# Moving the sums, the context and the next batch's x inside TensorE's order of a post-LN transformer block

## The reference

```python
q, k, v = split(x @ w_qkv)                      # 16 heads of 32
p   = softmax(q @ k.T / sqrt(512))              # all 1024 keys
x1  = layernorm(x + p @ v)
g   = fp4(x1) @ fp4(w_gate).T                   # 512 -> 1408
y   = fp4(x1) @ fp4(w_up).T
h   = silu(g) * y
out = layernorm(x1 + fp4(h) @ fp4(w_down).T)    # 1408 -> 512
```

## Time and profile before

| | us |
|---|---|
| median of 3 runs | 4034.84 (4033.22 to 4035.09) |
| the profiled execution | 4030.72 |
| its span | 4029.1 |
| set-up, up to the first weighing | 207.6 |
| one batch, from first weighing to first weighing | 478 to 480 |
| in it: first weighing to first gate of the FFN | 263 |

### The profile page before, as it was taken

How to read it: one execution, slowest core, us unless ns; L and a number is a source line. 1 busy time by engine, 2 the same in 40 slices (tenths; PEclk the granted TensorE clock), 3 DMA queues, 4 the chain that set the end, 5 groups by cost and what they waited for, 6 DMA issues and landing times. The chain is left out here.

```text
span 4029.1 us, 61264 instructions
## 1 busy us (share of the span) xinstructions
PE 3757.5 (93%) x22658; PEld 1726.6 (43%) x22853; DVE 3034.4 (75%) x4931; ACT 1711.7 (42%) x3085; POOL 2231.5 (55%) x1419
## 2 busy tenths in 40 slices
PE   3599999999999999999999999999999999999999
PEld 2243454334543445343444335433454344534344
DVE  9877787677866688667877778767786668866787
ACT  2166423653246622555226542356323552255522
POOL 1288523984258832687228852398425883268722
PEclk9699999999999999999999999999999999999999
DMA  4211101011011110101101110101101111011110
GB/s 164 79 35 33 53 22 36 17 42 47 24 30 29 36 45 19 40 26 33 48 24 36 33 53 19 38 17 41 48 24 31 29 36 45 19 38 27 33 48 22
DMA packets 106593, 152.83 MB, mean 38 GB/s; under 512 B 28176, under 2 KB 55568, under 8 KB 106128
## 3 DMA queue, kind: packets, MB, share of 16 engines
q1 hardware_dynamic: 106256, 148.49, 11.9%
HBM read 76.28 MB, written 19.66 MB: 24 GB/s over the span
## 5 line engine op out<-in xcount | busy, mean ns | idle before, releaser
L570 DVE TENSOR_REDUCE mx<-R 128x1 f32<-128x512 f32 x2080 | 1332.1, 685 | 567.3 <-PE R L662 561.0
L1191 ACT ACTIVATE arena<-SC 128x512 f32<-128x512 f32 x1344 | 747.8, 603 | 337.7 <-PE SC L1437 335.7
L1508 PE MATMUL SC<-wgu,split 128*128 128x512 f16 (+1 forms) x3456 | 715.9, 361 | 11.3 <-DVE split L1335 11.3
L1090 POOL TENSOR_TENSOR wd<-wd,arena 128x1024 f32<-128x1024 f32 x208 | 485.8, 2359 | 23.7 <-ACT arena L1191 22.6
L1116 POOL TENSOR_TENSOR arena<-arena,sc_h 128x704 f32<-128x704 bf16 (+2 forms) x136 | 176.1, 1312 | 577.0 <-DVE arena L495 577.0
L1508 PEld LDWEIGHTS SC<-wgu,split 128*128 128x128 f16 x3456 | 337.4, 98 | 345.6 <-DVE split L1335 13.2
L1191 ACT ACTIVATE wd<-SC 128x512 f32<-128x512 f32 x704 | 401.4, 604 | 195.9 <-PE SC L1437 185.6
L662 PE MATMUL R<-ks_even,qs_even 96*128 96x512 bf16 x1056 | 400.8, 395 | 57.1 <-issue 43.0
L1232 ACT ACTIVATE arena<-SC,gain 128x512 f32<-128x512 f32 (+1 forms) x192 | 125.0, 651 | 769.6 <-PE R L1508 396.2
L642 PE MATMUL R<-xT,wqkv 128*128 128x512 bf16 x1501 | 395.4, 381 | 28.9 <-DVE xT L557 14.8
L662 PE MATMUL R<-arena 96*128 96x512 bf16 x1024 | 373.8, 381 | 14.6 <-DVE xT L557 8.8
(11 more groups left out here) (138 smaller groups left out, 5332.1 us busy)
## 6 DMA issues: line engine op xcount, KB each, us to landing
x<-n_L_attn_embeddings_dram SPq DMA_DIRECT2D x136, 256.0 KB, 2.8
wd<-wd_kept SPq DMA_DIRECT2D x32, 512.0 KB, 5.1
out_dram<-x SPq DMA_DIRECT2D x64, 256.0 KB, 2.0
ks_even<-split SPq DMA_DIRECT2D x204, 64.0 KB, 2.0
qs_even<-split SPq DMA_DIRECT2D x408, 32.0 KB, 1.8
arena<-split SPq DMA_DIRECT2D x192, 64.0 KB, 2.0
arena<-split SPq DMA_DIRECT2D x384, 32.0 KB, 1.8
wd<-wd_kept SPq DMA_DIRECT2D x16, 384.0 KB, 6.9
```

Source lines behind the costliest of these rows:

```text
L570: nc.vector.reduce_max(mx[:, j:j + 1], ring_of(ring, job)[:, :], AX_X).then_inc(max_done, 1)
L1090: nc.gpsimd.tensor_tensor(acc[u % 2][i], first, probs_of(s)[:, hs, :], ALU.add).then_inc(pool_sum, 1)
L1191: nc.scalar.activation(probs_of(s)[:, hd, :], SC[e % SLOTS][:, :], ACT.Exp, scale=SCALE).then_inc(exp_done, 1)
L1508: last = nc.tensor.matmul(GU[kk % 2][which][:, 0:w], xhT[i % 2][:, part_x * KH + k, :], wgu[:, part_w * KH + k, which * I + first:which * ...
```

## The change

* The sum goes from step 1 to place 2 of step 2, ahead of the weighing; the turn of the sums from step 2 to ahead of the weighing of step 4, and the context's from step 3 to behind it. GpSimd's add follows one step later.
* The eight turns of the next batch's x go from one a step (steps 1 to 7 of unit 5, step 0 of unit 6) to two at a time, behind the weighings of steps 2, 4 and 6 of unit 5 and ahead of that of step 0 of unit 6. SyncE now loads all the tiles ahead of the maxima of unit 6.
* Two quarters of the last v projection go ahead of unit 7's last weighings; `neg` goes behind the turn of x's tile 0.
* First FFN tile: the turn of x tile 1 comes after the second chunk instead of the third; VectorE does the moments of tile 2 and the quantising of x tile 1 ahead of the context of unit 7, and quantises h by chunks, as the last tile does already; GpSimd follows.
* Set-up: the copy of w_down to HBM is issued after the last load of weights instead of between two of them.

```diff
--- before.py
+++ after.py
@@ -91,10 +91,10 @@
         ((3, (2, 3, 4)), (2, 2, 2, 1, 1, 1, 2, 1)), ((3, (5,)), (4, (0,)), (4, 0, 0, 0, 0, 1, 1, 2)),
         ((4, (1, 2, 3)), (0, 2, 2, 2, 2, 2, 2, 0)), ((4, (4,)), (1, 1, 1, 1, 0, 0, 0, 0)))
 SCORES_AT, VALUES_AT = (0, 1, 3, 4), 2
-SUM_STEP, SUM_T_STEP, CTX_STEP = 1, 2, 3
-ADD_TILE, ADD_TILE_LAST = 3, 2
+SUM_STEP, CTX_STEP = 2, 4
+ADD_TILE, ADD_TILE_LAST = 4, 3
 LN_MOMENTS, LN_SCALE = 5, 6
-X_TURNS = [(UNITS - 3, t) for t in range(1, TILES)] + [(UNITS - 2, 0)]
+X_TURNS = [(UNITS - 3, t) for t in (2, 2, 4, 4, 6, 6)] + 2 * [(UNITS - 2, 0)]
 def quarters(g, j):
@@ -115,23 +115,22 @@
     m = [("max", u + 1, n) for n in range(sum(counts[:t]), sum(counts[:t + 1]))]
     made, by_step = unit_projections(u)
     q = made[sum(by_step[:t]):sum(by_step[:t + 1])]
-    other = []
-    if u > 0:
-        other += [("sum", u - 1, 0)] if t == SUM_STEP else []
-        other += [("sumT", u - 1, 0)] if t == SUM_T_STEP else []
-        other += [("ctx", u - 1, 0)] if t == CTX_STEP else []
-    if (u, t) in X_TURNS:
-        other += [("xT", X_TURNS.index((u, t)), 0)]
+    before, behind = [], []
+    if u > 0 and t == SUM_STEP:
+        before = [("sum", u - 1, 0)]
+    if u > 0 and t == CTX_STEP:
+        before, behind = [("sumT", u - 1, 0)], [("ctx", u - 1, 0)]
+    turns = [("xT", n, 0) for n, step in enumerate(X_TURNS) if step == (u, t)]
     neg = [("neg", u + 1, 0)] if t == TILES - 1 and not ends else []
     if t == 0:
-        return m[0:1] + q[0:1] + m[1:2], m[2:3], [], m[3:4] + q[1:2], other, m[4:5] + q[2:] + m[5:]
-    return [], m[0:1] + q[0:1], m[1:2], neg + m[2:3] + other, m[3:4] + q[1:2], m[4:5] + q[2:] + m[5:]
+        return m[0:1] + q[0:1] + m[1:2] + turns, m[2:3], [], m[3:4] + q[1:2], [], m[4:5] + q[2:] + m[5:]
+    return [], m[0:1] + q[0:1], m[1:2] + before, turns + behind + neg + m[2:3], m[3:4] + q[1:2], m[4:5] + q[2:] + m[5:]
 def first_jobs():
     v = quarters(GROUPS, PROJ_JOBS - 1)
-    return ([("sum", UNITS - 1, 0), ("neg", UNITS, 0)] + v[0:2] + [("xhT", 0, 0)] + v[2:] + [("sumT", UNITS - 1, 0)],
+    return (v[0:2], [("sum", UNITS - 1, 0), ("xhT", 0, 0), ("neg", UNITS, 0)] + v[2:] + [("sumT", UNITS - 1, 0)],
             [("ctx", UNITS - 1, 0)])
@@ -139,7 +138,7 @@
     if i == 0:
-        return [], [], [("xhT", 1, 0)], []
+        return [("xhT", 1, 0)], [], [], []
     turns = [("hT", i - 1, n) for n in range(len(CHUNKS))]
     if i == TILES - 1:
         return turns[0:1], turns[1:2], turns[2:], [("hT", i, 0)]
@@ -349,12 +348,21 @@
         def pieces(i):
-            cols = H_PIECES if i < TILES - 1 else [chunk_cols(c) for c in range(len(CHUNKS))]
-            return [(len(H_PIECES) * i + n, c) for n, c in enumerate(cols)]
+            cols = [chunk_cols(c) for c in range(len(CHUNKS))] if in_chunks(i) else H_PIECES
+            before = len(H_PIECES) * i + (len(CHUNKS) - len(H_PIECES) if i > 0 else 0)
+            return [(before + n, c) for n, c in enumerate(cols)]
         def pieces_before(i, col):
-            return len(H_PIECES) * i + sum(c.start < col for _, c in pieces(i))
+            return pieces(i)[0][0] + sum(c.start < col for _, c in pieces(i))
+
+        def in_chunks(i):
+
+            return i in (0, TILES - 1)
+
+        def rounds_before(i):
+
+            return i + (len(CHUNKS) - 1 if i > 0 else 0)
         def chunk_cols(c):
             return slice(CHUNKS[c][0], CHUNKS[c][0] + CHUNKS[c][1])
@@ -800,8 +808,8 @@
                     if n == load_number[("round", DOWN_ROUNDS + 6)]:
                         for name in STACKS:
                             stack(GROUPS, name)
-                        sp.wait_ge(wT_done, 2 * DOWN_ROUNDS)
-                        sp.dma_start(wd_kept, wd[:, :, :]).then_inc(wd_saved, 16)
+                sp.wait_ge(wT_done, 2 * DOWN_ROUNDS)
+                sp.dma_start(wd_kept, wd[:, :, :]).then_inc(wd_saved, 16)
                 stack_maxima(UNITS)
                 stacks_done(sp, 1)
                 sp.wait_ge(m_loaded, 32)
@@ -1025,11 +1033,9 @@
                         if u == UNITS - 1:
                             stack(g, STACKS[2])
                         if u == UNITS - 3:
-                            for t in turns[:-1]:
+                            for t in turns:
                                 load_turn(t)
                         stack_maxima(u + 1)
-                        if u == UNITS - 3:
-                            load_turn(turns[-1])
                     def load_down(c):
@@ -1109,7 +1115,7 @@
                     def scale_h(i, n):
                         k, cols = pieces(i)[n]
-                        pool.wait_ge(rh_done, i + 1 + (n if i == TILES - 1 else 0))
+                        pool.wait_ge(rh_done, rounds_before(i) + 1 + (n if in_chunks(i) else 0))
                         if i >= 1:
                             pool.wait_ge(ring_full, ring.full(("hT", i - 1, (cols.stop - 1) // BANK)))
                         c = slice(cols.start // BLK, cols.stop // BLK)
@@ -1126,13 +1132,15 @@
                                 add(u - 1)
                     scale_x(0)
                     inverse_deviation("x", 1)
+                    inverse_deviation("x", 2)
+                    scale_x(1)
                     add(UNITS - 1)
                     for i in range(TILES):
-                        if i + 1 < TILES:
+                        if 1 <= i < TILES - 1:
                             scale_x(i + 1)
                         if 2 <= i < TILES - 1:
                             inverse_deviation("out", i - 2)
-                        if i + 2 < TILES:
+                        if 1 <= i < TILES - 2:
                             inverse_deviation("x", i + 2)
                         for n in range(len(pieces(i))):
                             scale_h(i, n)
@@ -1355,7 +1363,7 @@
                         first, w = CHUNKS[c]
                         dve.wait_ge(silu_done, k + 1)
                         if i >= 1 and c == 0:
-                            dve.wait_ge(rh_done, i)
+                            dve.wait_ge(rh_done, rounds_before(i))
                         nc.vector.scalar_tensor_tensor(h[:, first:first + w], GU[k % 2][1][:, 0:w], un_gain,
                                                        sg[:, k % 2, 0:w], ALU.mult, ALU.mult).then_inc(h_done, 1)
@@ -1367,26 +1375,31 @@
                         dve.wait_ge(y_added, i + 1)
                         moments("out", i, x1[:, i % 4, :], o_done)
+                    low_x(0)
                     maxima_transposed(UNITS)
-                    low_x(0)
                     reciprocals(UNITS - 1)
+                    first_moments(2)
+                    quantise_x(1)
                     context_out(UNITS - 1)
-                    for i in range(TILES - 1):
+                    for c in range(len(CHUNKS)):
+                        gated(0, c)
+                        if c == 1:
+                            low_x(1)
+                        dve.wait_ge(h_done, c + 1)
+                        quantise_h(0, chunk_cols(c))
+                    for i in range(1, TILES - 1):
                         gated(i, 0)
                         quantise_x(i + 1)
                         gated(i, 1)
-                        if i == 0:
-                            low_x(1)
-                        else:
+                        if i >= 1:
                             low_h(i - 1, 0)
                             if i >= 2:
                                 add_ffn(i - 2)
                                 second_moments(i - 2)
                             low_h(i - 1, 1)
                         gated(i, 2)
-                        if i >= 1:
-                            low_x(i + 1)
-                            low_h(i - 1, 2)
+                        low_x(i + 1)
+                        low_h(i - 1, 2)
                         if i + 2 < TILES:
                             if i == 2:
                                 dve.wait_ge(added, UNITS)
@@ -1489,6 +1502,7 @@
                                 weigh(s - 1)
                             if n in SCORES_AT:
                                 scores(u, t, SCORES_AT.index(n))
+                    run(first_jobs()[0])
                     weigh(len(steps) - 2)
                     weigh(len(steps) - 1)
@@ -1532,12 +1546,12 @@
                         if c == len(CHUNKS) - 1:
                             last.then_inc(y_done, 1)
-                    run(first_jobs()[0])
+                    run(first_jobs()[1])
                     for i in range(TILES):
                         places = tile_jobs(i)
                         gate_up(i, 0, 0)
                         if i == 0:
-                            run(first_jobs()[1])
+                            run(first_jobs()[2])
                         gate_up(i, 0, 1)
                         gate_up(i, 1, 0)
                         gate_up(i, 1, 1)
```

## The result

The changed kernel takes 3990.92 us, median of 4 runs (3987.16 to 3993.03), against 4034.53 for the kernel before (4 runs beside it): ratio 0.9891, 95% interval 0.9874 to 0.9908. That is 43.6 us faster; the forecast was 62.5 faster, 3972, in the range 3946 to 4005. The span of the profiled execution went from 4029.1 to 3985.5, also 43.6.

What follows compares the result with a forecast made beforehand. TensorE's order was taken as the bound. Per batch 1.3 + 0.6 - 1.1 + 1.7 + 4.5 = 7.0, by eight 56, plus 6.3 for set-up: 62.5 us off 4034.8, so 3972, range 3946 to 4005.

Steps and rivals of the forecast that it cites:

- pairs or first tiles worse: Outcome band 3984 to 4005 us, chance 0.22: x's pairs lose 3 a batch, or the first FFN tiles keep a wait.
- What bounds the kernel: TensorE's order, busy 93%; savings elsewhere count only for TensorE waits they end; in the set-up TensorE waits for VectorE.
- Part 1, the sums: Units 1 to 6: sums joined to weighings save 1.3 us a batch, and unit 1's GpSimd wait 0.6 more.
- The sign of 48 records in one run: Expected in the profile: sum and weighings in one run of 48 records with no bf16 between.
- the turns beside the weighing: Turns of sums and context at step 4: 0 to 0.09 us saved for each of eight, taken as 0.
- Part 2, x in pairs: Units 5 to 7: paired turns lose 4.9 us against 3.8 now, a loss of 1.1 a batch.
- the 4 to 5 given as a sign: Expected in the profile: TensorE's waits for xT fewer but longer, some 4 to 5 us a batch.
- Part 3 and 4, unit 7: Later add costs TensorE's maxima 0.4 us; quarters of v fill a 1.33 wait; gain 1.7 a batch, unit 7's sum included.
- Part 5: First FFN tiles: all three TensorE waits go, 4.8 us a batch, of which 4.5 taken.
- Part 6: Set-up: w_down's save behind the last weight load ends VectorE's wait for a load, 6.3 us once, bounds 0 and 6.5.
- The one on the pairs: Rival: the queue of x's pairs loses 3 us a batch instead of 1.1, 3987; shares a chance of 0.22.
- The exponentials held back by the sum: Rival: step 2's exponentials wait for the sum, 1.1 to 2.0 us a unit, up to 4084; chance 0.1.

Runs made afterwards that it cites:

- sums_only: Kernel before with only the sums, their turn and the context's moved next to the weighings and GpSimd's add a step later: 4033.36 us against 4033.32.
- sums_half: Kernel before with sums and context moved and maxima over 256 of 512 columns: 3970.26 us, against 3984.59 with the short maxima alone.
- x_only: Kernel before with only x's turns in pairs next to the weighings: 4033.60 us against 4033.32, ratio 1.0001.
- ffn_only: Kernel before with only the first FFN tiles' edits and two quarters of v ahead of unit 7's last weighings: 3981.99 us against 4033.32.
- ffn_save: Kernel before with the first FFN tiles' edits, the quarters of v and the later w_down copy, no moved sums, context or x: 3977.48 us against 4033.18.

## Why the prediction was right, and where it was not

The measured gain is 43.6 us where 62.5 were forecast, in the range but below the forecast's own band of 12 us. Per batch, the terms came out as follows: the sums with their wait 0.2 for 1.9 (units 1 to 4 and the 0.35 that sums_only shows for unit 6), x -1.2 for -1.1, unit 7 0.8 for 1.7, the FFN 5.1 for 4.5, and unit 0's scatter -0.3. In part it was luck that the time stayed so near: the misses of 1.7 and 0.9 were eased by 0.6 too little claimed for the FFN. The time lies in the band given to "pairs or first tiles worse", and neither was.

**What bounds the kernel** held: the gains and losses are found in the order of TensorE, as waits or, where they are short, as later starts. For the set-up the reading was loose. TensorE waits there for GpSimd, and GpSimd for VectorE; the chain still leads to VectorE.

**Part 1, the sums,** is the term that was mis-sized. 1.3 + 0.6 = 1.9 us a batch were forecast; sums_only measured 0.0 us in all. The cost of entering and leaving was right, as sums_half shows with 0.19 to 0.24 us in each of four units. The wrong step was to take the price of the burst as TensorE's gain without asking what its readers do with the time: I had worked that out for unit 5 alone and left it at 0 for the others, where 0.28 to 0.37 us go again in step 5 of units 1 to 4. The cover over the exponentials that I called thin was enough. The sign of 48 records in one run was miscounted: a sum has 16 and the weighing of two steps 16, so the run is of 32, as the timeline shows. For the turns beside the weighing I took 0, and the changed kernel's trace decides it. TensorE in unit 2, step 4:

```profile
1696.94 0.60 PE L692 MATMUL R<-identf,wd 128*128 128x128 f32 x4
1697.47 1.07 PE L1463 MATMUL CT<-wd,arena 128*32 128x512 f32 x8
1698.35 1.04 PE L1463 MATMUL CT<-arena 128*32 128x512 f32 x8
1699.32 0.66 PE L692 MATMUL R<-identf,wd 128*128 128x128 f32 x4
```

Four turns take 0.44 us, here the weighing starts 0.53 after the first: the 0.09 is paid. The weighings take 1.85 to the next turn, as alone, and the turn behind them 0.50 to the next maximum in sums_only, 0.06 more than the usual 0.44. The Trainium skill's rule of the drain at a change of tiling (TensorEngine Tiling (Array Packing), Key Properties) agrees.

**Part 2, x in pairs,** was right in size and place. Forecast for unit 5 of the changed kernel: 0.9 us late at the first bank and 2.0 lost up to the turn of sums, then a bank free at 3.4 and wanted at 1.8, 1.85 with what follows; in all a loss of 1.1 a batch. Measured in unit 5 of batch 4, from start to start: 0.89 and 1.97, then 1.71 (1803.71 less the score at 1801.78 is 1.93, less 0.22) and 1.87. Units 5 and 6 together are 0.84 longer, or 1.2 with the 0.35 taken off that sums_only shows for unit 6. The waits for xT add up to 2.8 us by the view, not to the 4 to 5 given as a sign, since much of the loss is in late starts too short for a bracket. That a pair alone costs nothing (x_only) I had not seen; my sum was for the combination and said so only in its wording.

**Part 3 and 4, unit 7:** 1.7 forecast, 0.81 measured. The quarters of v give their 1.3 alone (ffn_only). With the add a step later the first moments came 0.67 us later than before (forecast 0.4), counted from the unit's start, and the last score 0.50 later, of which 0.28 stood at step 4, ahead of the moments. So the quarters of v, which behind it fill the wait, push the last weighings 0.4 us past the last exponential. That part had been hidden in the wait that part 4 fills: two savings counted into one gap. GpSimd's last sums began within 0.1 us of before, as forecast. Its wait for the exponentials of step 2 was to stay under 1 us and was 0.8 to 1.6 in units 1, 2, 3 and 6 of batch 4, without a wait of TensorE behind it.

**Part 5** gave 5.06 against 4.5: all three waits went, and of the 0.3 kept back for small operations that GpSimd stretches nothing was needed. **Part 6** gave 6.6 against 6.3 in the changed kernel and 6.0 in the mean of all set-ups.

Of the rivals, none is the case alone. The one on the pairs named where the changed kernel loses most, unit 5, but its loss of 3 did not come. The exponentials held back by the sum did not hold TensorE.

What stays open: why unit 0 scatters, by 0.5 to 1.6 us within one execution of each kernel (it is 0.3 us longer after the change in the mean), why unit 6 gains 0.35 from the moved sums, more than the burst's 0.22, and how much of the loss in step 5 is the longer burst and how much the later context.

## What to carry to other kernels

Where a slower engine empties a ring behind the engine that sets the time, the slower one catches up while the other does work that needs no bank. Grouping that work saves the switch, 0.22 us here, but the saving is kept only if the reader can keep up behind the group: work out the reader's queue there, with every job that moves behind the group, before counting the saving. Several jobs in a row that hold banks belong where no other bank-holding job stands, and a wait that one edit fills can't also hide the delay that another brings: test each edit of a bundle alone, since here three of the five groups gave 56 us (ffn_save) and all five 44.

## What the runs showed of the hardware

Three things I had not expected. The way from a full-width fp32 turn into 32-column matmuls costs the same 0.09 us as from bf16, so here the type makes no difference. Halving the columns of a maximum made unit 5 2.1 us shorter, but unit 7 only 0.5 and unit 6 0.9, so VectorE's rate is most of the limit in unit 5 and less of it in units 6 and 7. And a DMA of 2816 KB ahead of a load in the same queue cost its reader 6.54 us, with an issue only 0.6 us earlier.
